# Layer 1 attention: the high parts of the probabilities against both halves of v in one product of 64 columns, the two results summed by VectorE

## The reference

```python
def _L1_attn_ref(x, w_attn, b_attn, w_proj, b_proj):
    B, T, C = (4, 512, 512)
    N_HEAD = 16
    HEAD_DIM = C // N_HEAD
    qkv = x @ w_attn + b_attn
    q, k, v = jnp.split(qkv, 3, axis=-1)
    ...
    att = jnp.einsum('bhqd,bhkd->bhqk', q, k) * scale
    att = jnp.where(causal, att, -jnp.inf)
    att = jax.nn.softmax(att, axis=-1)
    y = jnp.einsum('bhqk,bhkd->bhqd', att, v)
    y = y.transpose(0, 2, 1, 3).reshape(Bsz, Tlen, Cdim)
    return y @ w_proj + b_proj
```

## Time and profile before

| | us |
|---|---|
| median of 3 runs | 2140.75 (2137.35 to 2145.95) |
| the profiled execution | 2136.77 |
| its span | 2135.1 |
| TensorE busy | 1900.1 (89%) |
| VectorE busy | 1603.9 (75%) |
| ScalarE busy | 1362.1 (64%) |
| GpSimd busy | 1129.5 (53%) |

### The profile page before, as it was taken

One profiled execution on the slowest core, in us unless ns is written; L12 is line 12 of the kernel. 1 busy time (PEld: TensorE's weight loads), 2 busy tenths in 40 slices (PEclk: granted clock), 3 DMA queues, 4 the chain that ended last, 5 costly groups with the idle time before them and its releaser, 6 DMA issues. The chain is left out here.

```text
span 2135.1 us, 40247 instructions
## 1 busy us (share of the span) xinstructions
PE 1900.1 (89%) x14509; PEld 1183.6 (55%) x14509; DVE 1603.9 (75%) x3518; ACT 1362.1 (64%) x3320; POOL 1129.5 (53%) x877
## 2 busy tenths in 40 slices
PE   0779999999999999999999499957899999888999
PEld 0446556666666666666666255625666666643444
DVE  7789997788887887788865399947778787744760
ACT  6578777776777677777764144336868686855442
POOL 5677776766767766666650298733323232201440
PEclk9999999999999999999997799968999999999999
DMA  5334331222113212243212944375434343445000
GB/s 180 123 109 134 110 104 65 95 88 77 65 55 106 83 66 72 103 144 109 104 55 97 380 162 145 124 244 173 150 106 140 108 137 122 142 123 183 21 20 20
DMA packets 105757, 247.78 MB, mean 116 GB/s; under 512 B 10400, under 2 KB 39200, under 8 KB 103520
## 3 DMA queue, kind: packets, MB, share of 16 engines
q1 hardware_dynamic: 82768, 188.40, 25.9%
q10 hardware_dynamic: 19680, 46.67, 6.1%
q0 software_dynamic: 3120, 10.23, 1.6%
HBM read 174.21 MB, written 67.90 MB: 113 GB/s over the span
## 5 line engine op out<-in xcount | busy, mean ns | idle before, releaser
L996 PE MATMUL ps_q<-a_y,a_w 128*128 128x512 f16 x1536 | 343.5, 381 | 58.2 <-POOL a_y L691 57.5
L996 PEld LDWEIGHTS ps_q<-a_y,a_w 128*128 128x128 f16 x1536 | 147.7, 98 | 225.9 <-issue 60.5
L714 POOL TENSOR_TENSOR a_rb<-a_rb,router_y 128x512 f32<-128x512 f32 x128 | 181.0, 1414 | 167.3 <-ACT a_rb L857 166.5
L1210 DVE TENSOR_REDUCE a_nmax<-ps_s 128x1 f32<-128x512 f32 (+3 forms) x256 | 123.7, 483 | 113.6 <-PE ps_s L1017 113.4
L856 ACT ACTIVATE a_rb<-ps_q 64x512 f32<-64x512 f32 x128 | 76.0, 593 | 170.4 <-DVE a_ra L1195 168.9
L1043 PE MATMUL ps_o<-a_tt_,a_v 128*128 128x512 f32 (+3 forms) x512 | 161.2, 460 | 24.3 <-ACT a_tt_ L899 21.1
L1005 PE MATMUL ps_v<-a_w,a_y 128*128 128x128 f16 x3072 | 182.7, 220 | 0.0
L1005 PEld LDWEIGHTS ps_v<-a_w,a_y 128*128 128x128 f16 x3072 | 175.0, 98 | 1.2
L1065 PE MATMUL ps_v<-a_o,a_wo 128*128 128x512 f16 x732 | 168.0, 379 | 1.9 <-ACT a_v L883 1.9
L876 ACT ACTIVATE ps_s<-ps_s,a_nmax 128x512 f32<-128x512 f32 (+3 forms) x256 | 125.2, 489 | 41.7 <-DVE a_nmax L1212 41.6
L2210 ACT ACTIVATE a_ef<-ps,a_nmax 128x512 f32<-128x512 f32 (+3 forms) x256 | 131.7, 535 | 24.0 <-DVE a_nmax L2579 22.5
(11 more groups left out here) (346 smaller groups left out, 4975.1 us busy)
## 6 DMA issues: line engine op xcount, KB each, us to landing
a_w<-wqkv_split SPq DMA_DIRECT2D x48, 768.0 KB, 4.4
scratch_numlog<-wkv_nl ACTq DMA_DIRECT2D x40, 512.0 KB, 2.7
wkv_kt<-in_fT ACTq DMA_DIRECT2D x56, 256.0 KB, 2.6
router_y<-in_wqkv SPq DMA_DIRECT2D x16, 768.0 KB, 5.3
wqkv_split<-a_w SPq DMA_DIRECT2D x16, 768.0 KB, 6.8
a_stacks<-qk_parts SPq DMA_DIRECT2D x96, 128.0 KB, 2.5
gate_up<-in_gate_up SPq DMA_DIRECT2D x8, 1408.0 KB, 17.5
a_nlc<-scratch_numlog SPq DMA_DIRECT2D x17, 512.0 KB, 5.2
```

The costliest lines, as they stand in the source:

```text
L714: pool.tensor_tensor(rb[:, n, :], rb[:, n, :], rot[:, 2 * n + 1, :], ALU.mult).then_inc(s["roped"], 1)
L996: mm = pe.matmul(psq[n][:], w16[:, g % 2, wp, n, c, :], y16[b % 2][:, yp, c, :], start=c + m == 0, stop=c == CC - 1 and m == 2)
L1210: dve.tensor_reduce(nmax[:, 0, j:j + 1], cols(ps, j), AX, ALU.max, negate=True)
```

## The change

v16 is laid out as the earlier trace rows, so that the high and low 32 columns of a head lie side by side. For each of the 10 pairs the high exponentials meet both in one product of 64 columns; the low exponentials meet the high 32 columns in a second product, which adds to the first 32 of the 64. So a head has 20 products instead of 30, and its result takes 64 columns for each row tile, 256 in all. out first adds the two halves with a tensor_reduce over pairs that lie 32 columns apart, into a new tile both, waits for that (semaphore added) and multiplies both by the reciprocals. The high and low parts of v are written in runs of 32 columns.

```diff
-        v16 = sb("v16", [P, 2, 2, TT, P], F16)
+        v16 = sb("v16", [P, 2, TT, HPC, 2, D1], F16)
...
+        both = sb("both", [P, 2, TT, D1])
...
+        def v_of(q, part):
+
+            return v16[:, q % 2, :, :, part, :]
+
+        def by_head(v):
+            return v.rearrange("p t (i n) -> p t i n", i=HPC)
...
-                    pool.tensor_tensor(v16[:, q % 2, 1], vf[:], v16[:, q % 2, 0], ALU.subtract).then_inc(s["vlo"], 1)
+                    pool.tensor_tensor(v_of(q, 1), by_head(vf[:]), v_of(q, 0), ALU.subtract).then_inc(s["vlo"], 1)
...
-                    act.activation(v16[:, q % 2, 0], vf[:], ACT.Copy).then_inc(s["vhi"], 1)
+                    act.activation(v_of(q, 0), by_head(vf[:]), ACT.Copy).then_inc(s["vhi"], 1)
...
-                            for n, (tp, vp) in enumerate(PARTS):
-                                mm = pe.matmul(pso[:, j * D1:(j + 1) * D1],
+                            for tp, width in ((0, 2 * D1), (1, D1)):
+                                mm = pe.matmul(pso[:, j * 2 * D1:j * 2 * D1 + width],
                                                t16[:, i % 2, tp, bank, c0 + (j - m) * P:c0 + (j - m + 1) * P],
-                                               v16[:, q % 2, vp, m, i * D1:(i + 1) * D1],
-                                               start=m + n == 0, stop=m == j and n == 2)
+                                               v16[:, q % 2, m, i].rearrange("p a n -> p (a n)")[:, 0:width],
+                                               start=m + tp == 0, stop=m == j and tp == 1)
...
-                    dve.tensor_tensor(ob[:, q % 2, :, i * D1:(i + 1) * D1],
-                                      pso[:, 0:P].rearrange("p (t n) -> p t n", t=TT),
+                    if not isinstance(h, int) or h >= 2:
+                        dve.wait_ge(s["o"], h - 1)
+                    parts = pso[:, 0:2 * P].rearrange("p (t m n) -> p t m n", t=TT, m=2)
+                    dve.tensor_reduce(both[:, i % 2], parts.rearrange("p t m n -> p t n m"), AX,
+                                      ALU.add).then_inc(s["added"], 1)
+                    dve.wait_ge(s["added"], h + 1)
+                    dve.tensor_tensor(ob[:, q % 2, :, i * D1:(i + 1) * D1], both[:, i % 2],
                                       rsum[:, i % 2, :].unsqueeze(2).to_broadcast([P, TT, D1]),
                                       ALU.mult).then_inc(s["o"], 1)
```

More of the change, by code:

```diff
@@ L1901, in layer1_attn @@
             "bq", "qproj", "q", "q_hi", "kproj", "k", "k_hi", "qk_low", "parts_out", "stacked", "vproj", "vf", "vhi", "vlo", "scores", "nmax", "expd",
-            "turned", "thi", "tlo", "pv", "rsum", "o", "ot_ps", "ot_hi", "ot_lo", "proj", "x3", "x3_loaded", "x3_stored")}
+            "turned", "thi", "tlo", "pv", "added", "rsum", "o", "ot_ps", "ot_hi", "ot_lo", "proj", "x3", "x3_loaded", "x3_stored")}
         SCALE = float(np.float32(1.0) / np.sqrt(np.float32(D1)))
```

## The result

| | before | after |
|---|---|---|
| median, us | 2139.76 (20 runs) | 2148.72 (20 runs) |
| ratio to before | | 1.0047, 95% [1.0035, 1.0059] |
| profiled execution, us | 2136.77 | 2158.61 |
| its span, us | 2135.1 | 2156.7 |
| TensorE busy | 1900.1 | 1914.6 |

The changed kernel is about 9 us slower by the medians (10 by the ratio, with 7.5 to 12.6 in its interval), and the forecast was 2148.4. Its span is 2153.5. TensorE is busy longer with 640 products fewer, at a lower mean clock. Where the two traces of after agree, the reading belongs to the kernel; where they differ, it belongs to one execution.

A forecast was written before the change was run, and what follows sets the result against it. TensorE was taken to pace about half of a chunk, VectorE's queue the other half. 25 x 0.45 of VectorE's extra less 17 x 0.216 of TensorE's saving gave +7.6 on 2140.75: 2148.4 us, range 2132 to 2162.

The forecast's parts named there:

- Part 1, TensorE: TensorE's values block: 20 products instead of 30, a 64-column one at 29 ns, so 0.216 us saved a head.
- 17 counted heads: Heads in which TensorE's saving of 0.216 us was to shorten the time, 3.67 us in all.
- Part 2, VectorE: VectorE's out: reduction 0.41 us, wait 0.03, multiplication as before; 0.45 us more a head.
- rival B: VectorE's reduction costs by pairs, so 0.80 us more a head: +16.3, 2157.1 us; chance 0.17.
- with the multiplication from SBUF at what it cost from PSUM: VectorE's multiplication in out was to last as long from SBUF, leaving 0.45 us extra a head.
- counted slots: Slots where VectorE's extra 0.45 us was to count, mainly i = 2 and 3 of chunks 1 to 3; 25 heads.
- Part 3, the counts: Slot by slot, where each counts: VectorE's extra in 25 heads, TensorE's saving in 17; together +7.6 us.
- 25 heads: Heads of 64 in which VectorE's extra 0.45 us was to lengthen the time, 11.25 us in all.
- What would show it: Signs in the changed trace: blocks of 0.54 us, VectorE busy about 93 a batch, waits of 1.00 grown to 1.9.
- Rival C, the clock: TensorE's longer gaps bring four to eight more half-clock hits: +12 to +16.4, 2153 to 2157 us; chance 0.17.
- A: TensorE paces all, so its saving counts in all 64 heads: -13.8, 2127.0 us; chance 0.13, parts included.
- D: TensorE's saving and VectorE's extra both hidden, time unchanged: 2140 to 2143 us; chance 0.08.

The follow-up runs named there:

- wide_only: The changed kernel without the sum: out reads only the first 32 of each 64 columns, omitting high x low; 2135.3 us, 0.9989 of before.
- sum30_psum: The kernel before, 30 products kept, plus VectorE's sum written to PSUM and multiplied from there; 2146.0 us, 1.0032 of before.
- sum_in_psum: The changed kernel with the sum written to unused columns of the same PSUM bank and multiplied from there; 2142.2 us, 1.0018 of before.
- sum_only: The kernel before, 30 products of 32 columns kept, plus the change's reduction and multiplication on VectorE; 2154.6 us, 1.0074 of before.
- psum_twice: sum_in_psum with the reduction made twice, the first result unused; 2146.2 us, 1.0034 of before.
- after_again: The changed kernel unaltered, measured and profiled a second time against the kernel before; 2152.1 us, 1.0057.
- rows_before: The kernel before with two idle 128-row products ahead of each of three banks of a chunk's first-head scores; 2136.2 us, 0.9986.

## Why the prediction came out right, and where it didn't

The time was forecast within 0.3 us, and the sign and the bound (a packed VectorE, TensorE's saving mostly lost) hold. The closeness is luck in good part: the working lacks two terms of opposite sign (+6.6 and -3.6 where they count), and it stands on a median that was 1.0 too high.

**Part 1, TensorE.** Right: 0.21 saved a block (0.216 forecast), so a 64-column product costs about 29 to 30 ns. Its 17 counted heads, -3.7, compare with -2.8, -3.8 and -5.9 in the three pairs that differ mainly in this (before and wide_only, sum30_psum and sum_in_psum, sum_only and after; the last two across groups). Each pair is uncertain by some 4 to 6 us, so they confirm the order of the term and no more.

**Part 2, VectorE.** The reduction (0.39 against 0.41) and the wait on it (0.03 to 0.04 against 0.03) were right, so rival B is out: pairs 32 apart cost what 256 elements cost. The multiplication went from 0.25 to 0.29, and it does so with its input in PSUM as well, where it follows a reduction that it waits for. Added per head: 0.46 against 0.45.

The step that failed is "with the multiplication from SBUF at what it cost from PSUM". By its own duration the input's place makes no difference; by its neighbour it does. In 10 heads it cost 0.83 more: +8.3, of which 6.6 in counted slots, and 6.5 was measured (8.7 for the 9.2 of sum_only). The row that warned of it was the scan at 1613.43, 1.71 long where a scan of the same size takes 1.21, and one of the same line, five microseconds later at 1618.42, takes 1.27. GpSimd was at work beside the first.

**Part 3, the counts.** 25 heads by 0.46 would be 11.5. sum_in_psum costs 6.9 more than wide_only, and sum30_psum 7.5 more than before: 15 or 16 heads (for the second, whose interval is 3.2 to 10.7 us, 7 to 23). What is missing lies, at least in part, in the scans: in sum_in_psum and sum30_psum the 16 scans of line 295 are at 1.27 and those of line 276 at 1.23, since VectorE now comes to them when GpSimd is done or nearly so. That gives back 2.9 and 1.8, of it 3.6 in counted slots. 11.5 - 3.6 = 7.9, against 6.9 and 7.5 measured.

No run held the scans apart, but the traces show the term on the path. sum30_psum has the 30 products of the kernel before and the sum in PSUM, so between the two only VectorE's part differs. The wait for low parts behind the scan that was held up hardly grows, 1.00 to 1.03, with an exposed 0.46 in front of it and 0.44 of scan less:

```profile
1616.44 0.39 PE L2410 MATMUL ps<-a_stacks 96*128 96x512 f16 x1 [1.03 <-DVE a_t L2594]
```

And in stretches at clock 1.00 the terms can be added up. First, in the kernel before, the four heads in front of the 23.15: from slot i = 1 of chunk 0 to i = 0 of chunk 1, where the forecast counts nothing for VectorE. Then both stretches in sum30_psum; then the second one in sum_only and in psum_twice:

```profile
1678.41:1711.92 33.51, 31.70 (x326) 20.36 (x324) 23.31 (x50) 20.11 (x56) 7.83 (x7) 1.00 0.31 111
```

```profile
1680.57:1714.09 33.52, 31.70 (x327) 20.36 (x325) 24.51 (x54) 20.14 (x56) 7.37 (x7) 1.00 0.34 110
1714.09:1737.66 23.57, 21.34 (x278) 15.69 (x276) 20.70 (x47) 20.15 (x56) 7.36 (x7) 1.00 0.44 147
```

```profile
1719.39:1743.79 24.40, 21.34 (x279) 15.69 (x276) 21.52 (x47) 20.05 (x56) 7.36 (x7) 1.00 0.44 142
```

```profile
1708.69:1732.71 24.02, 20.70 (x239) 14.73 (x237) 21.93 (x51) 20.14 (x56) 7.35 (x7) 1.00 0.45 144
```

In the first stretch the sum costs nothing (33.51 to 33.52). In the second, where two heads are counted, the terms give, on 23.15: sum30_psum + 0.92 - 0.44 = 23.63 (measured 23.57); sum_only another 0.83, 24.46 (24.40); the changed kernel 24.25 (24.19); psum_twice, with one block saved and 2 x 0.32 more, 24.06 (24.02). So in these stretches the counts, the hold-up and the scan's relief all come out as priced. Over the whole stage they needn't: psum_twice would be 25 x 0.32 = 8.0 above sum_in_psum and measures 4.0, with 4 each way. If that is more than scatter, where it falls short isn't known.

**The sum redone**, in counted slots. +11.5 for the reduction, -3.7 for the products, -3.6 for the scans, +6.6 for the held-up multiplications: +10.8. Measured: +9.0 in the first comparison, +13.9 in the second, whose four runs leave about 5 us each way. Without the hold-up it is +4.2, and sum_in_psum measures 4.1. The forecast's +7.6 lacked the last two terms, and stood on a median that was 1.0 above that of the 20 runs.

**What would show it.** The products, the block, the reduction and VectorE's 93 a period came as said. The wait of 0.44 went to 0.66 (0.7 forecast, by one block's saving). That it is this saving and not the sum is shown by the same wait in wide_only and in sum30_psum:

```profile
1631.44 0.82 PE L2410 MATMUL ps<-a_qk 32*128 32x512 f16 x3 [0.65 <-DVE a_t L2593]
```

```profile
1634.73 0.82 PE L2410 MATMUL ps<-a_qk 32*128 32x512 f16 x3 [0.45 <-DVE a_t L2594]
```

The other waits fell short: 1.29 instead of 1.9, 0.74 instead of 1.2. A wait is the distance between two engines, and TensorE came later itself: that its lower clock did this is read from the blocks in front of the 1.29, not tested. Over the stage the waits for low parts (first row before, second after) rose by 4.1 only:

```profile
PE ps L2402 <- DVE a_t L2585: 19.4, 22, 3.4
```

```profile
PE ps L2410 <- DVE a_t L2593: 23.5, 27, 3.8
```

In after_again they are 29.0. The two periods were to grow by 0.9 and 1.8; they grew by 5.1 and 8.2 in after_again. Of this the hold-ups explain about 1.1 a period (three counted ones of 0.83, less three relieved scans of 0.44 to 0.50); the rest goes with the lower clock of these periods, and no run shows it apart.

**Rival C, the clock.** Open, and by the forecast's own sign a miss. The number of half-clock stretches in the stage was to grow by not more than three; in the profiles it goes from 8 to 22 and 19. One profile is a weak count, though: rows_before has 15, and wide_only has 16 and is no slower than before. The clock averaged over all runs shows the same more mildly, 20 us more at the lower level; at the 0.3 us each that the scatter of the runs gives, this would be 6 us. But the durations alone already add up to the measured time, so the two can't both count in full; that TensorE at the lower clock mostly uses up a wait for VectorE is argued from this, not shown. sum_in_psum has the same mean clock as after and is 6.5 us faster. What part of the 9 us is the clock's is not settled; fillers raised the clock without a measurable gain, which speaks for a small one.

**Rivals A and D** are out: A by wide_only, D by sum_only.

## What to carry to other kernels

When an operand moves from PSUM to SBUF, ask what the instruction then shares with other engines, and look in the trace for rows of the same shape with two durations: a scan of 1.71 beside one of 1.27 was the price list. An instruction inserted into a queue shifts all behind it against the other engines, so such a hold-up can vanish in one place and appear larger in another; cost it by where the neighbour's instruction starts. And a forecast that meets the median is tested by its terms: here undoing one term (the sum kept in PSUM) more than halved the loss (9.0 to 4.1 us by the medians).

## What the runs showed of the hardware that I had not expected

- A tensor_tensor of 128 columns with both inputs in SBUF took up to 1.12 us instead of 0.29 beside a GpSimd instruction of 1.15 that began 0.18 ahead of it; with one input in PSUM at the same place it took 0.29, in all of ten such places. A scan was held up in the same way, 1.71 instead of 1.27. The hold-up was a little shorter than what GpSimd still had to run when the instruction began: 0.83 of 0.97 for the multiplication at 1616.35, 0.44 of 0.62 for the scan at 1613.43.
- A multiplication from PSUM that waits for the instruction in front of it takes 0.29 (all 64 in sum_in_psum); without such a wait, started before its predecessor ended, it took 0.25 to 0.26 (60 of 64 in the kernel before; the other four, started 0.04 or more behind its end, took 0.29).
- Two idle products of 128 rows in front of scores that use 32 rows raised the mean granted clock from 0.958 and 0.959 to 0.962 and 0.961, with no gain in time that can be told.
